# Sharing the last batch's entry search among three engines, with other orders in the first batch and the last attention

## The reference

```
x = x + tanh(g_xattn) * attention(layernorm(x), ctx)
      # q = x Wq^T; k, v = ctx Wkv^T; 16 heads of 32, 64 keys, causal mask; softmax; Wout
x = x + tanh(g_ffn) * ffn(layernorm(x))
      # scores = softmax(x gate_w^T); the best 2 of 8 experts per token
      # y = sum over the two of weight * w2(silu(w1 x) * (w3 x))
      # z = the same with one shared expert (ws1, ws2, ws3) for all tokens
      # ffn = y + z
```

## Time and profile before

| what | value |
|---|---|
| median of 3 runs | 450.63 us (449.61 to 450.69) |
| profiled execution | 452.13 us, of which the span is 450.4 |
| PE, PEld busy | 414.9, 231.2 us |
| DVE, ACT, POOL busy | 306.4, 239.3, 229.6 us |
| mean granted clock | 0.986 |
| first expert's matmuls start | 260.32 us |

### The profile page before, as it was taken

One profiled execution on the slowest core, in us unless ns is written; L12 is line 12 of the kernel. 1 busy time (PEld: TensorE's weight loads), 2 busy tenths in 40 slices (PEclk: granted clock), 3 DMA queues, 4 the chain that ended last, 5 costly groups with the idle time before them and its releaser, 6 DMA issues.

```text
span 450.4 us, 8467 instructions
## 1 busy us (share of the span) xinstructions
PE 414.9 (92%) x2833; PEld 231.2 (51%) x2834; DVE 306.4 (68%) x663; ACT 239.3 (53%) x432; POOL 229.6 (51%) x206
## 2 busy tenths in 40 slices
PE   7989788999999999998987899999999999999980
PEld 7565445545546554464543455555555555555540
DVE  5989998888688876897869889844444444444430
ACT  2797784676647766855323448734344343434330
POOL 4019435636266762679343217565554646565422
PEclk9999999999999999998998999999999999999997
DMA  8940001706006075084343789575766666666543
GB/s 301 418 169 2 1 12 59 235 3 233 3 1 234 1 262 185 1 304 149 110 143 109 214 285 260 98 138 99 136 106 126 102 130 103 106 126 120 92 62 47
DMA packets 20769, 59.52 MB, mean 132 GB/s; under 512 B 3521, under 2 KB 3521, under 8 KB 20354
## 3 DMA queue, kind: packets, MB, share of 16 engines
q0 software_dynamic: 9504, 20.55, 25.4%
q1 hardware_dynamic: 11234, 38.56, 24.2%
HBM read 35.93 MB, written 23.17 MB: 131 GB/s over the span
## 4 chain that ended last, share of the span: by engine, by line
PE 61%; DVE 19%; POOL 7%; ACT 6%; issue 4%; another core or an unknown queue 1%; DMA 1%; POOLq 0%; DVEq 0%; ACTq 0%
PE bank L1671 46%; PE bank L1676 9%; DVE arena L1062 4%; POOL arena L590 3%; PE bank L1813 3%; POOL GT L615 2%; ACT arena L705 2%; DVE mv L1098 2%; DVE mx L1183 2%; ACT arena L753 1%; DVE xn L1152 1%; POOL ln L557 1%; PE bank L1824 1%; PE bank L1801 1%; DVE arena L1061 1%
## 5 line engine op out<-in xcount | busy, mean ns | idle before, releaser
L1671 PE MATMUL bank<-arena,GT 128*128 x468 | 107.4, 379 | 0.0
L689 POOL DMA_INDIRECT out<-rows,entry x39 | 62.7, 1609 | 65.9 <-issue 33.3
L1671 PE MATMUL bank<-arena,gT 128*128 (+1 forms) x336 | 80.2, 375 | 2.5 <-DVE x_sb L1282 1.3
L1671 PEld LDWEIGHTS bank<-arena,GT 128*128 128x128 f16 x468 | 45.8, 98 | 46.5
L705 ACT ACTIVATE arena<-bank 128x512 f16<-128x512 f32 (+1 forms) x88 | 48.5, 587 | 25.5 <-PE bank L1671 11.4
L666 POOL DMA_INDIRECT rows<-xrows,entry x39 | 38.9, 998 | 33.1 <-DVE entry L1462 11.3
L1062 DVE SCALAR_TENSOR_TENSOR arena<-bank,arena 128x512 f16<-128x512 f32 (+1 forms) x72 | 44.7, 663 | 12.4 <-ACT arena L705 7.5
L1671 PEld LDWEIGHTS bank<-arena,gT 128*128 128x128 f16 x336 | 32.5, 98 | 38.6 <-issue 3.2
L1061 DVE TENSOR_TENSOR gT<-bank,gT 128x256 f16<-128x256 f32 x55 | 23.0, 420 | 42.7 <-ACT gT L705 42.7
L1036 ACT ACTIVATE rows<-bank,weight 128x512 f32<-128x512 f32 x38 | 26.1, 687 | 38.0 <-PE bank L1671 38.0
L1627 DVE SCALAR_TENSOR_TENSOR uu<-th,bank 128x256 f32<-128x256 f32 x39 | 16.4, 421 | 43.4 <-ACT th L1003 42.8
(11 more groups left out here) (177 smaller groups left out, 675.2 us busy)
## 6 DMA issues: line engine op xcount, KB each, us to landing
x_sb<-in_experts SPq DMA_DIRECT2D x9, 768.0 KB, 6.1
rows<-in_experts SPq DMA_DIRECT2D x6, 768.0 KB, 6.3
xrows<-xn SPq DMA_DIRECT2D x16, 256.0 KB
out<-x_sb SPq DMA_DIRECT2D x16, 256.0 KB
image<-GT SPq DMA_DIRECT2D x5, 768.0 KB, 4.2
arena<-image SPq DMA_DIRECT2D x10, 384.0 KB, 4.0
x_sb<-in_x SPq DMA_DIRECT2D x1, 2048.0 KB, 16.8
x_sb<-in_x SPq DMA_DIRECT2D x2, 512.0 KB, 4.0
```

The costliest lines, as they stand in the source:

```text
L689: nc.gpsimd.indirect_dma_start(out=out, out_offset=bass.IndirectOffsetOnAxis(ap=entry[:, 1, j:j + 1], axis=0), in_=Y[:, j % RING, :], in_o ...
L1671: last = nc.tensor.matmul(dst, a, b, start=n == 0, stop=n == len(steps) - 1)
```

## The change

It touches four places. The core of the diff follows; semaphore names, GpSimd's and VectorE's renumbered groups and one bank that follows `out_bank` are left out. The lines between @@ say where one is.

1. First batch: four normalisation groups instead of three, the first two of two tiles; `own_block` moves from the start to behind the third `head_max`; key filling behind the third q; other orders of `exps`, `scores_out`, `head_sum`, `head_max`; statistics 12 to 15 behind the mix; `x1` and its statistics ahead of the second batch's first maximum.
2. Last attention: `ATTEND_LAST` is (2, 3, 0, 1); the output projection's banks follow it; hidden steps 2 and 3 of VectorE come behind all the probabilities; three clock-keeping products ahead of the attend.
3. Last feed-forward, who does what: ScalarE makes the weight's high half for 8 and the token's row for 5 (13 instructions), GpSimd the weight's low half for 8 and the token's row for 3 (11 instructions), VectorE keeps the comparisons (16).
4. Last feed-forward, orders: on VectorE, ScalarE and PE.

```diff
@@ orders, banks @@
...
-        ATTEND_LAST = (0, 2, 3, 1)
+        ATTEND_LAST = (2, 3, 0, 1)
...
+        def out_bank(b, i):
+            return mm_bank[ATTEND_LAST[i] if isinstance(b, int) and b == B - 1 else i]
         MIX_FIRST = (("q", 0), ("q", 1), ("v", 0), ("q", 2), ("p", 0), ("v", 1), ("q", 3), ("p", 1), ("v", 2),
@@ normalisation groups @@
...
-        LN1_GROUPS = ((0, PER), (PER, 2 * PER), (2 * PER, NT))
+        LN1_GROUPS = ((0, 2), (2, PER), (PER, 2 * PER), (2 * PER, NT))
@@ counts of products @@
...
         CONSTS = 24
-        HOTS = 3 * PER
+        ACT_TOKENS = 5
+        def act_sends(g):
+            return g + 1 + min(g + 1, ACT_TOKENS)
+        def pool_sends(g):
+            return g + 1 + max(g + 1 - ACT_TOKENS, 0)
@@ GpSimd, new function @@
...
+            def send_low():
+                pool.wait_ge(sent_step, 3)
+                for g in range(2 * PER):
+                    pool.wait_ge(row_hot, g + 1)
+                    pool.tensor_tensor(send[:, 2, g, :], in_row[:, g, :], sent[:, 1, g:g + 1].to_broadcast([P, P]),
+                                       ALU.mult).then_inc(low_sends, 1)
+                    if g >= ACT_TOKENS:
+                        pool.tensor_tensor(send[:, 0, g, :], in_row[:, g, :],
+                                           token[:, g % PER:g % PER + 1].to_broadcast([P, P]),
+                                           ALU.mult).then_inc(low_sends, 1)
             def softmax_mask(b):
@@ GpSimd, last_iteration @@
...
                 scatter_pairs(prev, (1,))
-            power1(1)
+                send_low()
+            power1(2)
             softmax_mask(0)
@@ ScalarE, send_lists @@
...
-            def send_lists():
+            def send_lists(g0, g1):
                 act.wait_ge(sent_step, 3)
-                for g in range(2 * PER):
+                for g in range(g0, g1):
                     act.wait_ge(row_hot, g + 1)
-                    for v in range(2):
-                        nc.scalar.activation(send[:, 1 + v, g, :], in_row[:, g, :], ACT.Copy,
-                                             scale=sent[:, v, g:g + 1]).then_inc(sends, 1)
+                    nc.scalar.activation(send[:, 1, g, :], in_row[:, g, :], ACT.Copy,
+                                         scale=sent[:, 0, g:g + 1]).then_inc(sends, 1)
+                    if g < ACT_TOKENS:
+                        nc.scalar.activation(send[:, 0, g, :], in_row[:, g, :], ACT.Copy,
+                                             scale=token[:, g % PER:g % PER + 1]).then_inc(sends, 1)
@@ ScalarE, last_feed_forward @@
...
                 tanh_h(f, 1)
+                send_lists(0, 3)
                 tanh_h(f, 2)
-                send_lists()
+                send_lists(3, 2 * PER)
+                got0_high()
+                turn_hi(c, "g", 0)
                 tanh_h(f, 3)
-                got0_high()
-                for i in range(PER):
+                for i in range(1, PER):
                     turn_hi(c, "g", i)
@@ ScalarE, iteration @@
...
                 if prev is None:
+                    exps(b, 0)
                     scores_out(b, 3)
-                    exps(b, 0)
                     exps(b, 1)
+                    exps(b, 2)
                 else:
...
                         project_hi(b + 1, n)
-                        if prev is None and n < 2:
-                            exps(b, n + 2)
+                        if prev is None and n == 0:
+                            exps(b, 3)
                     elif kind == "v":
@@ ScalarE, iteration, behind the attend @@
...
                     hi(aTv[:, 0, g, :], mm_bank[g][:, :], S_A / (S_P * S_KV)).then_inc(a_hi, 1)
-                scores_out(b + 1, 0)
                 if prev is None:
                     shared_hi_half(1)
+                scores_out(b + 1, 0)
                 scores_out(b + 1, 1)
@@ ScalarE, ahead of iteration(0) @@
...
             act.wait_ge(k_lo, NG)
+            project_hi(0, 2)
             fill_k(0)
-            project_hi(0, 2)
             project_hi(0, 3)
@@ VectorE, start @@
...
-            dve.wait_ge(ld_x0[0], 16)
-            statistics1(range(2))
-            dve.wait_ge(ld_x0[1], 16)
-            statistics1(range(2, PER))
-            aggregate1(0)
-            own_block()
+            for n in range(2):
+                dve.wait_ge(ld_x0[n], 16)
+                statistics1(range(2 * n, 2 * n + 2))
+                aggregate1(n)
             first_norm()
@@ VectorE, last_attention @@
...
                 head_sum(b, 2)
-                hidden(f, 2)
                 head_sum(b, 3)
-                router_logits(f)
                 for i in range(PER):
                     probabilities_lo(b, i)
+                router_logits(f)
+                hidden(f, 2)
                 hidden(f, 3)
@@ VectorE, blocks_hot @@
...
                 for g in range(2 * PER):
-                    V.tensor_scalar(send[:, 0, g, :], along16[:, :], spot[:, 1, g:g + 1], token[:, g % PER:g % PER + 1],
-                                    ALU.is_equal, ALU.mult).then_inc(hots, 1)
                     V.tensor_scalar(in_block[:, g, :], along16[:, :], spot[:, 0, g:g + 1], None,
@@ VectorE, last_feed_forward @@
...
                 turn_lo(c, "x2", 3)
+                router_logits(f)
                 turn_lo(f, "g", 2)
-                turn_lo(f, "g", 3)
-                router_logits(f)
                 router_choose(f, 0)
...
                 last_place(f)
+                rows_hot()
                 hidden(f, 1)
+                blocks_hot()
+                turn_lo(f, "g", 3)
                 base(f - 1, 1)
-                rows_hot()
-                blocks_hot()
                 pick_tiles()
@@ VectorE, iteration, start @@
...
                 if prev is None:
+                    head_sum(b, 0)
                     head_max(b, 3)
-                    head_sum(b, 0)
+                    head_sum(b, 1)
+                    statistics1(range(11, 12))
                 else:
@@ VectorE, iteration, mix @@
...
                         if prev is None and n < 2:
-                            head_sum(b, n + 1)
+                            head_sum(b, n + 2)
                     elif kind == "v":
                         values_lo(n)
-                        if n == 0:
-                            head_sum(b, 3)
                     else:
...
                             head_sum(b, 3)
-                        if prev is None:
-                            statistics1(((11, 12), (13,), (14,), (15,))[n])
                 if prev is None:
-                    aggregate1(2)
+                    statistics1(range(12, NT))
+                    aggregate1(3)
                 for g in range(NG):
@@ VectorE, iteration, behind the attend @@
...
                        gate_s[:, 0].rearrange("p c e -> p (c e)"), S_W).then_inc(gate_lo, 1)
-                head_max(b + 1, 0)
-                x1_and_statistics(b, 0)
-                if prev is None:
-                    bias1(2)
-                head_max(b + 1, 1)
-                x1_and_statistics(b, 1)
-                aggregate2(b, 0)
+                    x1_and_statistics(b, 0)
+                    head_max(b + 1, 0)
+                    bias1(3)
+                    x1_and_statistics(b, 1)
+                    aggregate2(b, 0)
+                    head_max(b + 1, 1)
+                else:
+                    head_max(b + 1, 0)
+                    x1_and_statistics(b, 0)
+                    head_max(b + 1, 1)
+                    x1_and_statistics(b, 1)
+                    aggregate2(b, 0)
                 norm2(b, 0)
@@ VectorE, ahead of iteration(0) @@
...
             V.tensor_scalar(gl[:, 1:2], gl[:, 3:4], 1.0 / (S_G * S_W), None, ALU.mult).then_inc(gates_ready, 1)
+            project_lo(0, 3)
+            turn_lo(0, "x", 0)
+            turn_lo(0, "x", 1)
             dve.wait_ge(gates_ready, 2)
...
             statistics1(range(8, 10))
-            project_lo(0, 3)
-            turn_lo(0, "x", 0)
-            turn_lo(0, "x", 1)
-            statistics1(range(10, 11))
             turn_lo(0, "x", 2)
             turn_lo(0, "x", 3)
-            for i in range(3):
-                head_max(0, i)
+            head_max(0, 0)
+            head_max(0, 1)
+            statistics1(range(10, 11))
+            head_max(0, 2)
+            own_block()
             iteration(0, None)
@@ TensorE, place_lists @@
...
                 for g in range(2 * PER):
-                    pe.wait_ge(hots, 2 * g + 2)
-                    pe.wait_ge(sends, 2 * g + 2)
+                    pe.wait_ge(hots, g + 1)
+                    pe.wait_ge(sends, act_sends(g))
+                    pe.wait_ge(low_sends, pool_sends(g))
                     last = nc.tensor.matmul(score_bank[1][:, 0:3 * P].rearrange("p (v r) -> p v r", v=3),
@@ TensorE, project_out @@
...
                     for u, v in ((0, 0), (0, 1), (1, 0)):
```

(30 more changed lines are left out.)

## The result

The changed kernel takes 451.95 us in the median (450.07 to 455.27) beside 450.69 of the kernel before on the same chip (448.89 to 453.45). The two medians differ by 1.26 us, 0.28%. The ratio over all runs of both kernels is 1.0045, with a 95% interval from 1.0026 to 1.0065, so the changed kernel is slower by 0.45%. Forecast was a gain, to 448.1; the time lies inside the range of 444.9 to 452.3, at its upper end.

A forecast was written before the change was run, and what follows sets the result against it. TensorE was busy 92% of the span, leaving about 35 us of waits and half-clock cost to win. 0.0 - 1.5 - 1.0 = -2.5 took the profiled 452.13 to 449.6, and the median, 1.5 lower, to 448.1; range 444.9 to 452.3.

The forecast's parts named there:

- (a): First batch: minus 0.6 us without the constants' move, 0.0 taken with it, ends of minus 0.6 and plus 1.9.
- the far end: First batch: cast waits for subtraction 2, the next operation for subtraction 3, till 40.1, 2.5 us in all; plus 1.9.
- Taken: 0.0: First batch: only the constants' cast waits, 0.6 us till subtraction 2 ends, cancelling the minus 0.6 of the other edits.
- (c): Last feed-forward: minus 1.0 us taken; minus 3.4 undisturbed, plus 1.25 if comparisons alternate with GpSimd's products.
- the slow rival: Everything alternates with GpSimd: first batch +1.9, last attention -1.5, last feed-forward +1.25, sum +1.65, 452.3 us; chance 0.17.
- (b): Last attention: minus 1.5 us taken; 0.0 if clock-keeping fails to hold the clock, a gain up to 1.9 possible.
- the two lengths that I offered for the comparisons: Last feed-forward, eight row comparisons on VectorE: 1.4 us if free, 4.6 us if alternating with GpSimd's products.
- the alternating one: Last feed-forward: each VectorE comparison alternates with a GpSimd product, rows ending near 246.1, plus 1.25 us; not taken.
- The clock should hold: Last feed-forward: down matmuls fill most of the 2.54 us wait, so the hidden matmuls are done 1.4 us earlier.
- The stall without a releaser: Last feed-forward: ScalarE's 3.76 us ahead of its g copies, left in place; the forecast is wrong if it moves onto the search.
- the rival of no net effect: Whole kernel: 449.3 to 452.0 us, from one wait in full, a clock fall, or GpSimd's dearest price; within 0.3%: 0.20.

The follow-up runs named there:

- own_back: The changed kernel with the three block constants moved back to the start, behind the second aggregation: 447.93 us, ratio to before 0.9959.
- first_undone: The changed kernel with the whole first-batch part undone, last attention and last feed-forward still changed: 449.51 us, ratio 0.9990.
- attn_alone: The kernel before with only the last attention's part of the change: 450.47 us, ratio 0.9976.
- rows_first: The kernel own_back with GpSimd's eleven products begun only after all eight row comparisons: 447.81 us, ratio 0.9934.

## Why the prediction was wrong, point by point

**(a), the step that failed.** The walk without the constants was good: minus 0.6 forecast, minus 0.5 measured (own_back against first_undone), the attend at 56.65 forecast and 56.84 measured. The constants were priced from both sides, and the far end, where the cast waits for the second subtraction and the next one for the third, is what happened, with the result that stood beside it: forecast plus 1.9, measured 2.4 minus 0.5 between fastest runs (1.5 at the last attention in the profiled execution). The two operations were held up by 2.48 us in all, for 2.5. What failed is the choice between the ends. "Taken: 0.0" rested on the earlier trace rows, one operation of 0.16 beside GpSimd's power, against the earlier trace rows, where a long subtraction ran beside the waiting one. The train in question was one of subtractions, so the earlier trace rows was the nearer row; in (c) the prediction took that same row for real, and in (a) only for one of the two operations.

The earlier trace rows was also read too kindly. The 0.16 us operation starts 0.07 into the power and not in the middle of it. And what tells the free operations from the held ones is GpSimd's instruction: the third tensor_scalar of the earlier trace rows, 0.17 us at 227.79, is free too, and it stands beside a power, where the two that waited stand beside subtractions:

```profile
227.26 0.73 POOL L557 TENSOR_TENSOR ln<-ln,minus_half 128x2 f32<-128x2 f32 x1 [5.34 <-DVE ln L1109]
```

The rule of the Trainium skill (SBUF — State Buffer, "SBUF: two separate sides") that was quoted against the change gives waits to the last operation, and to the cast if that runs in a fast mode, and none to what is neither in a fast mode nor reads two inputs from SBUF. The subtractions agree with it to 0.1 us in five operations and in every reduction. The power doesn't: a 0.16 us operation passes beside it in own_back too, at 8.56, inside a power from 8.42 to 9.22. Why the power lets it pass is open.

**(a), the term that was missing.** The prediction had it as a remark: TensorE would sit over 4 us before the first values and its clock could fall. It sat 3.45, and the clock fell behind that in three of the six traced executions, for 1.66 us. It had no price in the sum or in the slow rival.

**(b), mis-sized.** Minus 1.5 forecast; 1.9 in the profiled execution, 0.24 without the clock. The low halves ended at 210.09, where the forecast of 208.5 and the 1.5 brought along give 210.0, and the attend's 48 matmuls took 2.77 as forecast. But 1.7 of the gain was a fall that only some executions of before have; in the fastest runs attn_alone gained nothing.

**(c), mis-sized, with a wrong cover.** Minus 1.0 forecast, 2.15 in the profiled execution, 0.4 of it order and 1.4 clock. GpSimd's product takes 0.36 from start to start and 0.39 alone, not 0.49. Neither of the two lengths that I offered for the comparisons came: eight took 2.31, between 1.38 undivided and 4.6 alternating. The form was the alternating one that I had not taken:

```profile
L1444 DVE TENSOR_SCALAR rows<-along,spot x8: 247/415/439, 241.1 to 243.0; 128x128 f16<-128x128 f16 x8
L598 POOL TENSOR_TENSOR rows<-rows,sent x8: 392/394/431, 241.5 to 244.8; 128x128 f16<-128x128 f16 x8
```

Three comparisons of 0.25 pass before the first product starts. From the second product on, each comparison starts within 0.01 us of a product, one per product, and they stand 0.36 apart for 0.17 alone. It was cheap because the product is short and goes on at its 0.36. The block comparisons behind them took 2.09 for the same reason. pick_tiles wasn't stretched, since GpSimd had ended by then. "The clock should hold" was right at the counts, where the wait shrank from 2.54 to 0.49, and wrong 5 us later: the comparisons that now stand ahead of the hidden step made a new wait of 2.02 (1.10 of it remain in rows_first, where they aren't stretched), and the clock fell there instead, in all three executions above 453. The stall without a releaser stayed in its place, 3.75 us.

**The sum.** Minus 2.5 was forecast for the profiled execution and minus 2.0 came, with the parts wrong in both directions. The step from there to the median is the second error. I took away 1.5 because the profiled run lay so far above the median, and kept in (b) and (c) the 3 us of the same two falls. The falls can be counted once: either the gain is made against an execution that has them, or they are left out of both. That own_back's median of 447.93 lies beside the forecast of 448.1 is no support for the sum. Against the kernel before, its fastest run gained 1.1 us (448.80 to 447.66) and its median 2.65; the other 1.5 is falls that fewer of its runs have.

**The rivals.** The measured 451.95 lies in the rival of no net effect, 449.3 to 452.0, and its first condition, one of the two waits in full, is what happened. The slow rival's 452.3 is near by luck: its (a) came, its (c) of plus 1.25 did not, and falls of the clock stand in its place. Its sum had two slips. Three subtractions from 34.2 end at 39.8, not 40.1 (measured 39.32), and a gather at 255.05 with 6.99 us to the experts gives 262.04, plus 1.7 and not plus 1.25.

What stays open: why one execution has a fall at a given wait and another hasn't, with the same waits to 0.01 us before it.

## What to carry to other kernels

An operation of 0.2 us on VectorE costs up to a whole GpSimd instruction when it reads and writes SBUF in a form that waits for GpSimd (here a cast and an operation with two inputs, beside subtractions of 1.9 us); put it where GpSimd is idle, or where VectorE waits anyway, and check what runs beside the new place and not only what slack the old one had. Before a stage's gain is counted, take the part that is clock out of it, and compare executions with the same falls; the fastest runs of two kernels show what the order is worth, the medians show what the waits do to the clock. A long wait on TensorE can have a second price, and steps that keep it busy, no longer than the wait, bought 1.7 us of the median here.

## What the runs showed of the hardware

- A cast and a 128x1 scalar_tensor_tensor in SBUF wait for the end of the GpSimd subtraction in flight: 1.10 to 1.76 us beside subtractions of 1.9. Beside a train of products the comparisons go one per product, 0.36 apart for 0.17 alone, and the products keep their pace. Reductions, statistics and operations that read a PSUM bank don't wait, and beside GpSimd's power of 0.7 to 1.05 us neither did the scalar_tensor_tensor (0.16) nor an int32 tensor_scalar (0.17).
- GpSimd does a 128x128 product of 16-bit numbers in 0.39 us, 0.36 from start to start, less than the 0.52 and 0.49 that the slope between its 128x384 and 128x1024 subtractions of 32-bit numbers gave.
- Twelve matmuls of 2.75 us take 4.44 with the clock at its lower level in part of them. The falls came behind waits of 1.7 to 3.5 us, in some executions of the same kernel and not in others.
- The same kernel's profiled execution lay 0.0 to 1.8 us off its median, so the difference of two profiled executions can have the other sign than that of the medians, as it had here.
